# State space layer: one scan over both states in the odd chunks too, with the second state's carried value added to its first drive column

## The reference, cut to what matters

```python
dt = jax.nn.softplus(dt_r @ W_dt + b_dt)
A = -jnp.exp(A_log)
dA = jnp.exp(dt[..., None] * A)               # decay of each channel, state and token
dBx = (dt * xc)[..., None] * Bm[:, :, None, :]  # drive
def step(h, inp):
    dA_t, dBx_t, C_t = inp
    h = h * dA_t + dBx_t
    y = jnp.einsum('ben,bn->be', h, C_t)
    return (h, y)
y = jnp.moveaxis(ys, 0, 1) + xc * D
y = y * jax.nn.silu(z)
return y @ W_out
```

## Time and profile before

| | us |
|---|---|
| median of 3 runs | 3282.31 |
| lowest, highest | 3278.56, 3284.23 |
| span of the profiled execution (the profile lists no other time of it) | 3282.5 |
| state space layer, first scan to last | 40.8 to 1022.3 |
| PE, DVE, ACT, POOL busy over the span | 2918.6, 2077.4, 1409.4, 1502.3 |

### The profile page before, as it was taken

How to read it: one execution, slowest core, us unless ns; L and a number is a source line. 1 busy time by engine, 2 the same in 40 slices (tenths; PEclk the granted TensorE clock), 3 DMA queues, 4 the chain that set the end, 5 groups by cost and what they waited for, 6 DMA issues and landing times. The chain is left out here.

```text
span 3282.5 us, 43728 instructions
## 1 busy us (share of the span) xinstructions
PE 2918.6 (89%) x15459; PEld 1876.9 (57%) x15459; DVE 2077.4 (63%) x3809; ACT 1409.4 (43%) x2698; POOL 1502.3 (46%) x1189
## 2 busy tenths in 40 slices
PE   6898898898887679799999999988886999999998
PEld 2343343343334565455555555546665888888887
DVE  7899899898998646566666666647883222222222
ACT  5667767757753302254545454545551111111111
POOL 5787787787784541233333333236763111111111
PEclk8999999999989689899999999989997999999999
DMA  7135135135130171122222222220114665565662
GB/s 228 59 97 155 59 99 155 60 96 155 64 102 0 67 244 41 28 47 49 53 65 59 49 49 49 47 72 14 47 53 171 190 207 178 190 206 177 186 211 61
DMA packets 280263, 339.71 MB, mean 103 GB/s; under 512 B 84547, under 2 KB 237311, under 8 KB 280047
## 3 DMA queue, kind: packets, MB, share of 16 engines
q1 hardware_dynamic: 256799, 303.41, 31.0%
q0 software_dynamic: 16704, 27.21, 3.5%
q10 hardware_dynamic: 6544, 6.30, 0.6%
HBM read 231.55 MB, written 104.80 MB: 102 GB/s over the span
## 5 line engine op out<-in xcount | busy, mean ns | idle before, releaser
L542 POOL TENSOR_TENSOR mb_drive<-mb_dtx,mb_b_rep 128x1024 f32<-128x1024 f32 x255 | 597.2, 2356 | 191.0 <-DVE mb_pD L439 94.8
L853 PE MATMUL mb_pY<-mb_hc,ident 128*128 128x512 f32 x1024 | 509.4, 624 | 53.3 <-DVE mb_hc L456 53.1
L1969 DVE TENSOR_REDUCE at_nm_of<-at_pS 128x1 f32<-128x128 f32 x756 | 402.5, 555 | 201.5 <-PE at_pS L1961 108.8
L3126 POOL DMA_INDIRECT out<-et_y,et_to x71 | 111.9, 1577 | 659.9 <-DVE et_y L3180 402.5
L3170 DVE TENSOR_TENSOR et_mT<-et_silu,et_pU 128x512 f32<-128x512 f32 (+1 forms) x160 | 100.4, 628 | 470.8 <-ACT et_silu L3141 470.8
L853 PEld LDWEIGHTS mb_pY<-mb_hc,ident 128*128 128x128 f32 x1024 | 193.8, 198 | 330.4 <-issue 188.4
L3141 ACT ACTIVATE et_silu<-et_pG 128x512 f32<-128x512 f32 (+1 forms) x160 | 87.8, 549 | 651.0 <-PE et_pU L3202 651.0
L1957 PE MATMUL at_pS<-at_kT,at_qT 64*128 64x128 f32 x756 | 301.4, 446 | 71.1 <-DVE at_nm_of L1969 61.1
L598 ACT ACTIVATE mb_pD<-mb_dt,mb_a_neg 128x512 f32<-128x512 f32 x384 | 259.6, 688 | 154.5 <-DVE mb_hc L456 143.2
L439 DVE TENSOR_TENSOR_SCAN mb_pD<-mb_pD,mb_drive 128x1024 f32<-128x1024 f32 x128 | 292.8, 2288 | 46.6 <-ACT mb_pD L596 44.5
L445 DVE TENSOR_TENSOR_SCAN mb_pD<-mb_pD,mb_carried,mb_drive 128x512 f32<-128x512 f32 x256 | 314.4, 1273 | 7.6 <-ACT mb_pD L598 7.6
(11 more groups left out here) (491 smaller groups left out, 5292.6 us busy)
## 6 DMA issues: line engine op xcount, KB each, us to landing
t_wg<-in_t_wgT SPq DMA_DIRECT2D x40, 1024.0 KB, 6.2
t_wu<-in_t_wuT SPq DMA_DIRECT2D x40, 1024.0 KB, 8.9
t_wd<-in_t_wdT SPq DMA_DIRECT2D x40, 1024.0 KB, 11.3
mb_b_rep<-mb_rows SPq DMA_DIRECT2D x64, 512.0 KB, 5.7
...
```

The source lines that it names most:

```text
L542: nc.gpsimd.tensor_tensor(drive[G % RINGS][:, :, :], dtx[:, m, :].unsqueeze(1).to_broadcast([P, 2, CH]), b_rep[:, 2 * j:2 * j + 2, :], ALU ...
L853: last = nc.tensor.matmul(pY[:, :], K.ident[:, :], hc[G % RINGS][:, k, :], start=False, stop=(j == PAIRS - 1 and k == 1))
L1969: nc.vector.tensor_reduce(nm_of[:, w0 // 512, a, qb:qb + 1], score_bank(t, k)[:, 0:w1 - w0], axis=AX.X, op=ALU.max, negate=True).then_inc( ...
```

## The change

In odd chunks too, both states go through one scan of 1024 columns. It starts from `carried` of the first state. The second state's column 0 has decay zero, so its carried value has to come in by another way: ScalarE adds exp(a * dt[0]) * carried to column 0 of the second state's drive, in place (an ACTIVATE with function Identity, scale and bias from a column each). The factors exp(a * dt[0]) of all 16 states of a block, `opening`, are made once for a block by one small exp. The new ACTIVATE waits for `opening`, for `carried` (s_keep) and for the drive of the item from GpSimd (s_drv), for which ScalarE did not wait before; it is what now releases the scan.

```diff
--- before.py
+++ after.py
@@ -273,13 +273,13 @@
         b_rep, c_rep = sb("b_rep", [P, NST, CH]), sb("c_rep", [P, NST, CH])
         drive = [sb(f"drive{q}", [P, 2, CH]) for q in range(RINGS)]
         hc = [sb(f"hc{q}", [P, 2, CH]) for q in range(RINGS)]
-        carried = sb("carried", [P, ME, NST])
+        carried, opening = sb("carried", [P, ME, NST]), sb("opening", [P, ME, NST])
         yz_all = sb("yz", [P, ME + 1, CH])
         pD = [K.ps(c, f"mb_pD{q}", [P, 2, CH]) for q in range(RINGS)]
         pA, pY = K.ps(c, "mb_pA", [P, CH]), K.ps(c, "mb_pY", [P, CH])
         rows_dram = [nc.dram_tensor(f"mb_rows{q}", [2 * NST, CH], F32).ap() for q in range(2)]
 
-        s_cw, s_relu, s_next = sem("cw"), sem("relu"), sem("next")
+        s_cw, s_relu, s_next, s_opening = sem("cw"), sem("relu"), sem("next"), sem("opening")
         s_w, s_in, s_x1, s_x2, s_a, s_set, s_diag, s_stats, s_mv, s_veps, s_rstd, s_xn = (
             sem(n) for n in ("w", "in", "x1", "x2", "a", "set", "diag", "stats", "mv", "veps", "rstd", "xn"))
         s_A, s_read, s_cv, s_xc, s_gate, s_abs, s_e, s_t, s_ln, s_log, s_dt, s_dtx = (
@@ -433,17 +433,12 @@
                 ch, m, j = of(G)
                 r = G % RINGS
                 eng.wait_ge(s_drv, G + 1)
-                if ch % 2 == 0:
-                    eng.wait_ge(s_dec, 2 * G + 2)
-                    both = lambda T: T[r][:, :, :].rearrange("p k t -> p (k t)")
-                    nc.vector.tensor_tensor_scan(both(pD), both(pD), both(drive), 0.0, ALU.mult, ALU.add).then_inc(s_scan, 2)
-                    return
-                if G % ITEMS in (0, RINGS):
+                if ch % 2 and G % ITEMS in (0, RINGS):
                     eng.wait_ge(s_keep, ch // 2 * ITEMS + (ITEMS - RINGS if G % ITEMS == 0 else ITEMS))
-                for k in range(2):
-                    eng.wait_ge(s_dec, 2 * G + k + 1)
-                    nc.vector.tensor_tensor_scan(pD[r][:, k, :], pD[r][:, k, :], drive[r][:, k, :],
-                                                 carried[:, m, 2 * j + k:2 * j + k + 1], ALU.mult, ALU.add).then_inc(s_scan, 1)
+                eng.wait_ge(s_dec, 2 * G + 2)
+                both = lambda T: T[r][:, :, :].rearrange("p k t -> p (k t)")
+                before = carried[:, m, 2 * j:2 * j + 1] if ch % 2 else 0.0
+                nc.vector.tensor_tensor_scan(both(pD), both(pD), both(drive), before, ALU.mult, ALU.add).then_inc(s_scan, 2)
 
             def weigh(G):
                 ch, m, j = of(G)
@@ -591,11 +586,22 @@
                         back = of(G - RINGS)[0]
                         if back % 2 == 0:
                             eng.wait_ge(s_keep, back // 2 * ITEMS + (G - RINGS) % ITEMS + 1)
-                if k == 1 and ch % 2 == 0:
-                    nc.scalar.activation(pD[r][:, 1, 1:], dt[:, m, 1:], ACT.Exp, scale=scale)
-                    nc.scalar.copy(pD[r][:, 1, 0:1], zeros[:, 0:1]).then_inc(s_dec, 1)
-                else:
-                    nc.scalar.activation(pD[r][:, k, :], dt[:, m, :], ACT.Exp, scale=scale).then_inc(s_dec, 1)
+                if k == 0:
+                    nc.scalar.activation(pD[r][:, 0, :], dt[:, m, :], ACT.Exp, scale=scale).then_inc(s_dec, 1)
+                    if j == 0 and ch % 2:
+                        nc.scalar.activation(opening[:, m, :], a_neg[:, m, :], ACT.Exp, scale=dt[:, m, 0:1]).then_inc(s_opening, 1)
+                    return
+                nc.scalar.activation(pD[r][:, 1, 1:], dt[:, m, 1:], ACT.Exp, scale=scale)
+                blank = nc.scalar.copy(pD[r][:, 1, 0:1], zeros[:, 0:1])
+                if ch % 2 == 0:
+                    blank.then_inc(s_dec, 1)
+                    return
+                n = 2 * j + 1
+                eng.wait_ge(s_opening, ch // 2 * ME + m + 1)
+                eng.wait_ge(s_keep, ch // 2 * ITEMS + G % ITEMS + 1)
+                eng.wait_ge(s_drv, G + 1)
+                nc.scalar.activation(drive[r][:, 1, 0:1], opening[:, m, n:n + 1], ACT.Identity, scale=carried[:, m, n:n + 1],
+                                     bias=drive[r][:, 1, 0:1]).then_inc(s_dec, 1)
 
             def transposed(ch, k):
                 eng.wait_ge(s_A, use(f"LN{k}", ch))
```

## The result

The changed kernel is slower. In the first comparison (13 runs of each on one chip) it took 3295.45 us in the median (3285.29 to 3301.62) against 3279.17 (3266.32 to 3287.24): ratio 1.0045 [1.0033 to 1.0057] (a ratio's 95% interval stands in square brackets), 14.7 us more by the ratio and 16.3 by the medians. In a second one on another chip (12 runs against 23) it took 3290.52 against 3284.60: ratio 1.0019 [1.0004 to 1.0034], 6 us more. The forecast was 3281, with no measurable change as the likeliest case.

A forecast was written before the change was run, and what follows sets the result against it. VectorE was taken to set the layer's pace, TensorE close behind. Chunk terms 0 + 1.6 + 0.4 - 1.2 gave +0.8 us, likeness to even chunks -3.3; the middle, -1.3 from 3282.5, gave 3281, range 3270 to 3292.

The forecast's parts named there:

- 0.13 was taken: VectorE's saving per odd item from the joined scan: 0.13 us, between 0.085 and 0.17; 16 us over 128 items.
- forecast 51 and 4: New ScalarE work: 51 us for zero columns and sums in four chunks, some 4 us for the exps of `opening`.
- at the places named: VectorE's longer waits for ScalarE ahead of scans: in odd chunks behind s = 4, 9, 21 and 26.
- forecast 1.2: Chunk 7: two scans behind lumps start 1.4 us later, then 20 scans save 2.6; net -1.2 us.
- the one on chunks 1, 3 and 5: These chunks end about 1.6 us later before waits absorb it; counted as 0, +1.6 and +0.4 us.
- what was gained or lost before is wiped out here: Chunk 3: `finish` waits 2.67 us for TensorE, whose work is unchanged, so earlier gains or losses vanish.
- absorbs the 1.6 wholly and down to 0.4: Chunks 1 and 5 end in waits of 2.45 and 1.21 us for ScalarE, which cover the 1.6 us delay.
- the lump of s = 21: Lump of ScalarE work in chunk 3; the scan behind it starts at least 1.0 us later (0.6 and 0.4).
- VectorE sets the pace of the layer: State space layer: VectorE is busy 112 us of 120 to 124 in even chunks, 117 of 122 to 125 in odd.
- The loss: Rival: ScalarE waits inside decays for GpSimd's drives, four times a chunk, delaying TensorE; 13 us, 3295 us; chance 0.20.
- waits for those copies: Within the loss: TensorE, busy 110 of 122 us, waits for ScalarE's copies from `pA`, queued behind the stalled decay.
- The gain: Rival: waits behind the lumps do not grow; 16 to 22 us go, 3261 to 3272, likeliest 3266; chance 0.22.

The follow-up runs named there:

- late4: The whole kernel before, with four idle VectorE instructions (some 4.5 us) behind the layer's last weigh: 3295.66 against 3294.62 us, ratio 1.0003.
- layer_before: The kernel before, cut off behind the state space layer, whose result is stored: 1042.2 us (1039.3 to 1047.3).
- after: Profile trace of the whole changed kernel; 853.4 us from the first scan of chunk 1 to the last weigh, against 850.1 before.
- after_again: The whole changed kernel once more, against the kernel before: ratio 1.0019.
- extras_layer: Layer before, odd scans still in two, with the new small ScalarE instructions beside them, sums unread but waited for: 1051.8 us.
- the changed layer: The changed kernel cut off behind the state space layer: 1050.5 us, in a second set of runs 1051.2.
- split_all: Whole kernel before, with a scan per state in even chunks too and no zero column there: 3290.85 us, ratio 0.9990.
- lumps_layer: The changed layer with items 0, 7, 18, 24, 28 to 31 of odd chunks scanned in two as before: 1039.7 us.
- lumps_even_layer: The code of lumps_layer with items 7, 24, 28, 29, 30 of even chunks scanned in two as well: 1042.4 us.
- nodrive_layer: extras_layer whose sum reads a constant and does not wait for GpSimd's drive: 1051.3 us.
- quiet_layer: extras_layer with the new small instructions only at the 24 odd-chunk items outside 0, 7, 18, 24, 28 to 31: 1040.7 us.
- lumps_cut: The same code as lumps_layer, run on another occasion: 1039.1 us (1035.0 to 1040.0).
- edge_cut: The changed layer with only item 0 of odd chunks scanned in two as before: 1050.5 us (1046.3 to 1051.5).

## Why the prediction was wrong

**What held.** An odd item's period is 175.33 - 171.94 = 3.39 us after, by the starts of two scans, against 3.49: 0.10 saved where 0.13 was taken, inside the bounds of 0.085 and 0.17. ScalarE's busy time grew by 1461.1 - 1409.4 = 51.7 us, forecast 51 and 4. VectorE's wait for ScalarE ahead of the scans went from 52 to 75 us (34.0 + 40.9), forecast 70 or more, at the places named. Chunk 7 came out 0.5 us shorter (113.37 to 112.83), forecast 1.2; against late4's trace (114.2) it is 1.4. The sum took 0.39 us where 0.3 was taken; that lies inside its bounds. The estimate from the Trainium skill ("ScalarE: Activation LUTs", What ACT_TABLE_LOAD costs), 0.37, was nearer, and the trace agrees with it at 0.386.

**The step that failed** is the one on chunks 1, 3 and 5: "what was gained or lost before is wiped out here" at the wait of `finish`, and the last wait of the chunk "absorbs the 1.6 wholly and down to 0.4". Three things were wrong in it.

It took waits for TensorE as fixed cover. The trace of the prediction has 2.67 us at `finish` in chunk 3, but 1.03 in chunk 1 and 3.94 in chunk 5, and it waits 2.45 and 1.21 at two chunk ends. With the same instructions late4's chunk 1 has 1.03 at `finish` and no wait at the end, and takes 120.4 us where that chunk took 123.5 (granted clock 1.00 against 0.97). First the trace of the prediction, chunks 1 and 5, then late4:

```profile
269.66 0.69 DVE L461 TENSOR_TENSOR mb_yz<-mb_yz,mb_pY 128x512 f32<-128x512 f32 x1 [1.03 <-PE mb_pY L853]
...
763.94 0.69 DVE L461 TENSOR_TENSOR mb_yz<-mb_yz,mb_pY 128x512 f32<-128x512 f32 x1 [3.94 <-PE mb_pY L853]
```
```profile
267.09 0.69 DVE L461 TENSOR_TENSOR mb_yz<-mb_yz,mb_pY 128x512 f32<-128x512 f32 x1 [1.03 <-PE mb_pY L855]
...
289.98 2.30 DVE L439 TENSOR_TENSOR_SCAN mb_pD<-mb_pD,mb_drive 128x1024 f32<-128x1024 f32 x1
```

So the cover was there in some executions only, and the layer that the sum started from was 7 us longer than late4's. Between its own two traces the sum was not far off: chunks 1, 3, 5 and 7 came to 0.8 + 3.6 - 2.0 - 0.5 = +1.9 us, forecast +0.8. It was the starting trace that was not typical. Such a wait may also be no store of time to draw on, since TensorE itself waits for ScalarE's copies, and what delays ScalarE can move the end of the wait as well. (That the delay goes by way of those copies is read from the order of the instructions; no run took a copy away.)

It mis-sized the end of the chunk. Counted from the chunk's first scan, the scan behind the lump of s = 21 moved by 90.80 - 89.58 = 1.2 us in chunk 3, forecast 1.0 or more; `finish` came 0.3 earlier, so there the cover held; the scan of item 29 moved by 113.11 - 111.64 = 1.5, forecast 1.8. But the next chunk moved by 3.6 and not 1.6 (the forecast's own terms, 1.8 less three items at 0.13, give 1.4). Items 30 and 31 and the next chunk's first scan were to run at VectorE's pace; they wait 0.54 + 1.08 + 0.66 = 2.3 us for ScalarE, which had not caught up. In late4's chunk 1, without a wait at the end, the scan of item 29 starts at 109.8 and the next chunk at 120.4; in the changed chunk 5 at 111.4 and 123.0: +1.6 and +2.6.

It left out the even chunks. Item 0 of the odd chunk behind each waits 1.15 to 1.34 us, and at a granted clock of 0.97 even chunks take 120.9 and 121.5 us before (layer_before2, late4, chunk 2) and 122.9 to 123.3 after (after, chunk 4; after_again, chunks 2 and 4).

Behind all three stands "VectorE sets the pace of the layer", which was true of its busy share only. extras_layer and the changed layer differ by 13 us in VectorE's work (its scans are busy 315.0 and 300.4 us in the odd chunks) and have the same new work on ScalarE: 1051.8 us and 1050.5 to 1051.2. split_all, lumps_layer and lumps_even_layer change VectorE's work by 1 to 10 us, and none of them moves the time by more than 4.

**The rivals.** The loss, 3295 us, had the time but not the cause: ScalarE does stand inside the decays for GpSimd's drive, 1.76 us where 1.2 was worked out, but once in each of chunks 1, 3 and 5 (twice in chunk 7) and not four times, and nodrive_layer prices it at nothing. That its time was near the first comparison's is luck. Its point, that TensorE "waits for those copies", may hold for the 0.54 us that every item adds to ScalarE's queue without any such wait; that is not shown. The gain is refuted.

## What to carry to other kernels

Here an edit had to be priced on the engine that works in lumps, and at its lumps: half a microsecond of small instructions at 8 items of 32 cost more there than the same at the 24 others, and more than the faster scans gave. Before a wait is counted as cover for a delay, ask whether what ends the wait depends on the engine that is delayed. And time the stage alone, in several runs, before building a sum of 1 us terms on one trace of it.

## What the runs showed of the chip

**The same layer, 8 to 12 us apart, with the granted clock.** The runs of most cut kernels line up by their mean granted clock (share of the 2.4 GHz level; the other level is 1.2 GHz). The layer before: 1047.2 us at 0.946, 1042.2 and 1044.7 at 0.952, 1039.0 and 1039.3 at 0.959, 1036.5 at 0.961. quiet_layer: 1048.0 at 0.952, 1042.3 at 0.959, 1035.6 at 0.965. About 1 us for each 0.001 to 0.002. lumps_cut does not follow it: 1035.0 to 1040.0 at 0.956 and 0.957. At the same clock the changed layer stays slower: 1050.6 to 1052.1 at 0.951 and 0.952, 1048.7 at 0.957. extras_layer has 1051.8 to 1052.4 at 0.952. So the change's 8 to 9 us aren't made by the clock; but quiet_layer at 0.952 is 1048.0 and its low median owes something to its better clock (0.960 in the mean of its runs, against 0.955 for the layer before on the same chip). At about 0.959 the layer before takes 1039.2, quiet_layer 1042.3 and extras_layer 1046.8 (at 0.958): 3 us for the 24 items and 4.5 for the eight. By the same measure edge_cut, 1050.2 to 1051.5 at 0.947 to 0.949 and 1046.3 at 0.955, gains some 3 us on the changed layer. Why a kernel gets the better clock was not tried.

**Prices.** A scan of 1024 columns that starts from a column takes 2347 ns, from a constant 2288. Two of 512 instead of one cost an item 0.05 us more with constants (split_all, 3.37 against 3.32) and 0.10 with columns (3.49 against 3.39). An ACTIVATE of one column with scale and bias from columns takes 386 ns and holds the next one back by 0.29; an exp of 16 columns with a column as scale 0.29 us (L592); a copy of one column 0.15, and the next starts 0.08 behind it.
